# Mixture-of-experts layer after attention: every handoff of the expert pipeline one round apart, and eight result buffers

## The reference

```python
logits = x @ gate_weight.T                      # 128 tokens here per block, 1024 in all
probs = softmax(logits)
routing_weights, selected_experts = top_k(probs, 8)
routing_weights = routing_weights / routing_weights.sum(-1)
for each expert e:                              # 64 experts, I = 96, H = 256
    gate, up = split(x @ gate_up_weights[e])    # 256 -> 2 * 96
    out = (silu(gate) * up) @ down_weights[e]   # 96 -> 256
    final += combine[:, e] * out
x = x + final
```

## Time and profile before

| | us |
|---|---|
| median of 3 runs | 521.24 |
| lowest and highest | 520.41, 523.81 |
| span of the profiled execution | 576.6 |
| expert pipeline in the profile | about 325 to 547 |
| of it, full rounds back to back | 365 to 529 |
| reading back and adding, storing | 547 to 576.6 |
| PE, DVE, ACT, POOL busy | 477.4, 342.7, 305.9, 212.3 |

### The profile page before, as it was taken

One profiled execution on the slowest core, in us unless ns is written; L12 is line 12 of the kernel. 1 busy time (PEld: TensorE's weight loads), 2 busy tenths in 40 slices (PEclk: granted clock), 3 DMA queues, 4 the chain that ended last, 5 costly groups with the idle time before them and its releaser, 6 DMA issues. The chain is left out here.

```text
span 576.6 us, 10371 instructions
## 1 busy us (share of the span) xinstructions
PE 477.4 (83%) x3073; PEld 351.1 (61%) x3073; DVE 342.7 (59%) x1204; ACT 305.9 (53%) x854; POOL 212.3 (37%) x224
## 2 busy tenths in 40 slices
PE   4586999999899899999983766987988888888666
PEld 1366767877787678788653423765665666655322
DVE  4768496596685894795793564544355454553033
ACT  3456787885966887779864201333244343444200
POOL 0344110041114631025584642245444455445600
PEclk9799999999999999999996788999899899899879
DMA  8920862000301102002998739884444444330097
GB/s 283 411 70 19 167 131 74 1 1 0 76 1 54 69 30 73 2 1 74 345 404 291 278 107 298 227 288 129 111 115 115 113 128 127 107 95 13 19 363 304
DMA packets 47318, 79.49 MB, mean 138 GB/s; under 512 B 8266, under 2 KB 31127, under 8 KB 46880
## 3 DMA queue, kind: packets, MB, share of 16 engines
q1 hardware_dynamic: 36864, 55.34, 31.1%
q0 software_dynamic: 7680, 16.93, 8.2%
q10 hardware_dynamic: 2720, 6.55, 3.5%
HBM read 56.54 MB, written 26.44 MB: 144 GB/s over the span
## 5 line engine op out<-in xcount | busy, mean ns | idle before, releaser
L620 POOL DMA_INDIRECT pair_rows<-eout,dest x93 | 91.8, 987 | 99.5 <-ACT eout L634 78.2
L833 ACT ACTIVATE sact<-ps 128x192 f32<-128x192 f32 (+1 forms) x50 | 16.3, 325 | 122.7 <-remote 73.6
L1323 DVE SCALAR_TENSOR_TENSOR aact<-sact,wcol,ps 128x96 f32<-128x96 f32 x96 | 26.0, 311 | 92.6 <-issue 87.1
L1685 PE MATMUL ps<-wts,xg 128*64 (+1 forms) x512 | 71.5, 342 | 3.7 <-DVE copy_gu L1346 2.2
L691 ACT ACTIVATE lg<-lg,mneg 128x128 f32<-128x128 f32 (+1 forms) x128 | 56.4, 443 | 26.1 <-DVE mneg L1029 21.5
L1685 PEld LDWEIGHTS ps<-wts,xg 128*64 128x64 f32 x512 | 53.0, 143 | 16.5 <-issue 9.5
L541 POOL DMA_INDIRECT slot_rows<-rows,pair_slot x48 | 47.9, 998 | 37.2 <-issue 24.1
L1512 PE MATMUL ps<-oT,wo_sb 128*128 128x256 f32 x240 | 54.4, 380 | 0.0
L1706 PE MATMUL ps<-wts,aT 96*64 96x256 f32 (+1 forms) x256 | 49.8, 395 | 4.4 <-issue 3.4
L1512 PEld LDWEIGHTS ps<-oT,wo_sb 128*128 128x128 f32 x240 | 44.6, 190 | 6.2 <-ACT oT L634 0.7
L634 ACT ACTIVATE lg<-lg,rinv 128x128 f32<-128x128 f32 (+1 forms) x128 | 45.9, 448 | 2.5 <-issue 1.7
(11 more groups left out here) (237 smaller groups left out, 1184.4 us busy)
## 6 DMA issues: line engine op xcount, KB each, us to landing
wts<-in_experts_dram SPq DMA_DIRECT2D x22, 640.0 KB, 8.0
xrow<-slot_rows SPq DMA_DIRECT2D x192, 65.0 KB
pairs<-pair_rows SPq DMA_DIRECT2D x16, 512.0 KB, 11.2
wts<-in_experts_dram ACTq DMA_DIRECT2D x10, 640.0 KB, 6.1
slot_rows<-zero SPq DMA_DIRECT2D x1, 4160.0 KB, 24.2
wT<-in_wq_t_dram SPq DMA_DIRECT2D x4, 512.0 KB, 6.5
wq_raw<-in_wq_l_dram SPq DMA_DIRECT2D x1, 2048.0 KB, 14.6
wo_sb<-in_wo_l_dram SPq DMA_DIRECT2D x1, 2048.0 KB, 20.5
```

The lines of the kernel that those rows point to most:

```text
L620: nc.gpsimd.indirect_dma_start(out=pair_d, out_offset=bass.IndirectOffsetOnAxis(ap=dest[:, d:d + 1], axis=0), in_=out_rows(d), in_offset=N ...
L1685: ins = nc.tensor.matmul(ps[h * R:(h + 1) * R, 2 + u % 2, k * I2:(k + 1) * I2], xg[u % len(xg)][:, k, cc, h * R:(h + 1) * R], moving, star ...
```

## The change

The computation, the tiles and the weights stay. What changes is which round each step belongs to, the order within an iteration, and the buffers that this needs. PE now does, group by group in turns, `turn_rows` of round g and `gate_up` of g - 1, then `turn_act` of g - 2, then `down` of g - 3. ACT does `silu` of g - 1, `copy_turned` and `copy_down` of g - 2, `copy_out` of g - 3. DVE does for each group `copy_turned_rows`, `copy_gate_up` and `weigh`, and `find_rows` of both groups at the end. There is one more iteration. `sact` has two buffers; from the ninth group on `gate_up` goes through three PSUM banks (5, 2, 3) in turn, and `turn_act` through one bank (4) for the whole round; results have eight buffers instead of six.

```diff
-    NOUT = 6
+    NOUT = 8
...
+        round_of = {g: r for r, gs in enumerate(ROUNDS) for g in gs}
...
+        PLAIN = 8
+
+        def gu_bank(u):
+            return 2 + u % 2 if u < PLAIN else (5, 2, 3)[(u - PLAIN) % 3]
+
+        def gu_before(u):
+            return u - 2 if u < PLAIN else u - 3
...
             def copy_turned(a):
-                act.wait_ge(at_done, a + 1)
+                act.wait_ge(at_done, ROUNDS[round_of[a]][-1] + 1)
...
             def silu(u):
                 act.wait_ge(gu_done, u + 1)
-                if u >= 1:
-                    act.wait_ge(act_ready, u)
+                if u >= 2:
+                    act.wait_ge(act_ready, u - 1)
...
-            for g in range(NR + 2):
+            for g in range(NR + 3):
                 us = ROUNDS[g - 1] if 1 <= g <= NR else []
-                outs = ROUNDS[g - 2] if g >= 2 else []
-                for a in outs:
-                    copy_turned(a)
+                outs = ROUNDS[g - 2] if 2 <= g < NR + 2 else []
                 for u in us:
                     silu(u)
                 for a in outs:
+                    copy_turned(a)
+                for a in outs:
+                    copy_down(a)
+                for a in ROUNDS[g - 3] if g >= 3 else []:
                     copy_out(a)
-                for u in us:
-                    copy_down(u)
...
             for g in range(NR + 1):
                 ins_ = ROUNDS[g] if g < NR else []
-                for x in ins_:
-                    copy_turned_rows(x)
-                    find_rows(x)
                 us = ROUNDS[g - 1] if g else []
                 for k in range(max(len(us), len(ins_))):
+                    if k < len(ins_):
+                        copy_turned_rows(ins_[k])
+                        copy_gate_up(ins_[k])
                     if k < len(us):
                         dve.wait_ge(dest_ready, us[k] + 1)
                         weigh(us[k])
-                    if k < len(ins_):
-                        copy_gate_up(ins_[k])
+                for x in ins_:
+                    find_rows(x)
...
             def turn_act(a):
                 pe.wait_ge(act_ready, a + 1)
-                if a >= 2:
-                    pe.wait_ge(at_copied, a - 1)
-                if a == TABLE_AT:
-                    pe.wait_ge(cols_read, 2)
+                if a == ROUNDS[round_of[a]][0] and a:
+                    pe.wait_ge(at_copied, a)
...
             def gate_up(u):
-                if u >= 2:
-                    pe.wait_ge(act_ready, u - 1)
+                if u == PLAIN:
+                    pe.wait_ge(cols_read, 2)
+                if gu_before(u) >= 0:
+                    pe.wait_ge(act_ready, gu_before(u) + 1)
...
-            for g in range(NR + 2):
-                outs = ROUNDS[g - 2] if g >= 2 else []
+            for g in range(NR + 3):
...
-                for x in ROUNDS[g] if g < NR else []:
-                    turn_rows(x)
-                for a in outs:
+                xs = ROUNDS[g] if g < NR else []
+                us = ROUNDS[g - 1] if 1 <= g <= NR else []
+                for k in range(max(len(xs), len(us))):
+                    if k < len(xs):
+                        turn_rows(xs[k])
+                    if k < len(us):
+                        gate_up(us[k])
+                for a in ROUNDS[g - 2] if 2 <= g < NR + 2 else []:
                     turn_act(a)
-                for u in ROUNDS[g - 1] if 1 <= g <= NR else []:
-                    gate_up(u)
-                for a in outs:
+                for a in ROUNDS[g - 3] if g >= 3 else []:
                     down(a)
```

More of the change, by code:

```diff
@@ L214, in adaln_attn_ffn @@
         o = 16 * KIB
-        xg = [at(f"xg{i}", [P, 2, CC, P], off) for i, off in enumerate((take(2 * KIB), take(2 * KIB), r3 + 10 * KIB, rows_off[0] + NOUT * KIB))]
+        xg = [at(f"xg{i}", [P, 2, CC, P], off) for i, off in enumerate((take(2 * KIB), take(2 * KIB), r3 + 10 * KIB, rows_off[0] + (NOUT - 2) * KIB))]
         wcol = at("wcol", [P, (NE + MORE) // 2], take(384))
-        sact = at("sact", [P, 2, I], take(2 * I * 4))
+        sact = [at(f"sact{i}", [P, 2, I], off) for i, off in enumerate((take(2 * I * 4), row_off + 2 * KIB))]
         aact0 = take(2 * I * 4)
@@ L233, in adaln_attn_ffn @@
         assert o <= spare + 5 * KIB
-        eout = at("eout", [P, NOUT, C], rows_off[0])
+        eout_pair = [at(f"eout{i}", [P, 2, C], off) for i, off in enumerate([rows_off[0] + 2 * i * KIB for i in range(NOUT // 2 - 1)] + [row_off])]
         eout_first = at("eout_first", [P, 3, C], r3 + 12 * KIB)
@@ L822, in copy_turned @@
                 n = len(GROUPS[a])
-                act.wait_ge(at_done, a + 1)
+                act.wait_ge(at_done, ROUNDS[round_of[a]][-1] + 1)
                 if a >= 2:
                     act.wait_ge(dn_done, a - 1)
-                copy(aT[a % 2][0:I, 0:n, :], ps[0:I, 4 + a % 2, 0:n * P].rearrange("p (k t) -> p k t", k=n)).then_inc(at_copied, 1)
+                copy(aT[a % 2][0:I, 0:n, :], ps[0:I, 4, a % 2 * 2 * P:(a % 2 * 2 + n) * P].rearrange("p (k t) -> p k t", k=n)).then_inc(at_copied, 1)
             def silu(u):
@@ L830, in silu @@
                 act.wait_ge(gu_done, u + 1)
-                if u >= 1:
-                    act.wait_ge(act_ready, u)
-                nc.scalar.activation(sact[:, 0:n, :], ps[:, 2 + u % 2, 0:n * I2].rearrange("p (k i) -> p k i", k=n)[:, :, 0:I],
+                if u >= 2:
+                    act.wait_ge(act_ready, u - 1)
+                nc.scalar.activation(sact[u % 2][:, 0:n, :], ps[:, gu_bank(u), 0:n * I2].rearrange("p (k i) -> p k i", k=n)[:, :, 0:I],
                                      ACT.Silu).then_inc(silu_done, 1)
@@ L845, in copy_out @@
                 else:
-                    copy(eout[:, d % NOUT:d % NOUT + n, :], ps[:, 6 + a % 2, 0:n * C].rearrange("p (k c) -> p k c", k=n)
+                    copy(eout_pair[d % NOUT // 2][:], ps[:, 6 + a % 2, 0:n * C].rearrange("p (k c) -> p k c", k=n)
                          ).then_inc(out_copied, 1)
@@ L1322, in weigh @@
                 for k, d in enumerate(GROUPS[u]):
-                    ins = V.scalar_tensor_tensor(out=aact[u % 2][:, k, :], in0=sact[:, k, :], scalar=wcol[:, d:d + 1],
-                                                 in1=ps[:, 2 + u % 2, k * I2 + I:(k + 1) * I2], op0=ALU.mult, op1=ALU.mult)
+                    ins = V.scalar_tensor_tensor(out=aact[u % 2][:, k, :], in0=sact[u % 2][:, k, :], scalar=wcol[:, d:d + 1],
+                                                 in1=ps[:, gu_bank(u), k * I2 + I:(k + 1) * I2], op0=ALU.mult, op1=ALU.mult)
                 ins.then_inc(act_ready, 1)
@@ L1644, in turn_act @@
                 pe.wait_ge(act_ready, a + 1)
[L1645 to L1648 removed]
+                if a == ROUNDS[round_of[a]][0] and a:
+                    pe.wait_ge(at_copied, a)
                 for k in range(len(GROUPS[a])):
[L1650 removed]
+                    ins = T_(ps[0:I, 4, (a % 2 * 2 + k) * P:(a % 2 * 2 + k + 1) * P], aact[a % 2][:, k, :])
                 ins.then_inc(at_done, 1)
@@ L1684, in gate_up @@
                                 moving = copy_gu[m % NCOPY][:, cc * I2:(cc + 1) * I2]
-                            ins = nc.tensor.matmul(ps[h * R:(h + 1) * R, 2 + u % 2, k * I2:(k + 1) * I2],
+                            ins = nc.tensor.matmul(ps[h * R:(h + 1) * R, gu_bank(u), k * I2:(k + 1) * I2],
                                                    xg[u % len(xg)][:, k, cc, h * R:(h + 1) * R], moving, start=(cc == 0), stop=(cc == CC - 1))
```

3 lines of the change are left out of this document (1 added, 2 removed).

## The result

Before: 521.4 us (median of 4, 520.41 to 523.81). After: **541.42 us** (median of 4, 540.07 to 542.75). The ratio is 1.034, interval 1.028 to 1.041: the change makes the kernel 20.0 us slower. The forecast was 536, in a range of 513 to 543.

What follows compares the result with a forecast made beforehand. The prediction took TensorE's own sequence of instructions to bound the timed rounds. From 521.2 us it added 12.8 for TensorE's order, took off 1 for handoffs and added 3.4 for the end: 536.4, say 536 us, range 513 to 543.

Steps and rivals of the forecast that it cites:

- The sum: Whole kernel: 521.2 + 12.8 for order, - 1 for handoffs, + 3.4 for the end, giving 536.4, say 536 us.
- Rival A: Faster: late completions are in timed runs too, looser handoffs regain idle time and switches lie in it; 511.5 us, chance 0.15.
- B: No change: another resource, likely SyncE's loads, sets rounds of about 6.5 us, only the end counts; 524.6 us, chance 0.17.
- Part 1: TensorE's order: six changes of form a round instead of two, 0.145 us each; rounds of 6.52 us, +12.8 us.
- Part 2: Handoffs: TensorE's waits for aact and copy_gu go, mostly absent from timed runs; -1 us, ends 0 and 4.9.
- Part 3: VectorE and ScalarE: same instructions reordered, later find_rows may delay row loads; 0, at worst 2 us.
- Part 4: End of the kernel: results leave one round later, last twelve scatters run back to back; +3.4 us, ends 0 and 6.

Runs made afterwards that it cites:

- before again: The kernel before, unchanged, run and profiled again; its profiled execution took 523.75 us, its group's median was 524.32 us.
- four further: The changed kernel, with TensorE alternating by double tile from the sixth iteration on, ten changes of form a round instead of six; 552.34 us, ratio 1.056.
- the buffers alone: The changed kernel with the old orders on all three engines, keeping its result and silu buffers and PSUM banks; 525.16 us, ratio 1.000.
- the alternation alone: The kernel before with only turn_rows and gate_up alternating by group on TensorE, four changes of form a round; 527.43 us, ratio 1.005.
- the depth alone: The changed kernel without alternation, turn_act ahead of gate_up, find_rows directly behind copy_turned_rows, down still of round g - 3; 533.93 us, ratio 1.019.
- The run without alternation: The changed kernel, but TensorE does turn_rows of both groups, then gate_up of both; four changes of form a round; 537.77 us, ratio 1.022.
- the run with two switches: The changed kernel, but TensorE does turn_rows of both groups, turn_act, gate_up of both, down; two changes of form a round; 535.55 us, ratio 1.021.
- the exception: The kernel before with turn_rows and gate_up alternating by group in the first eight iterations only; start 30.7 us, 523.64 us, ratio 0.998.
- the run with early copies: The changed kernel, with ScalarE copying a group's results directly behind copy_turned, ahead of the copies of down weights; 537.18 us, ratio 1.025.
- the run with the end first: The changed kernel, but from iteration NR - 2 on down and copy_out of round g - 3 stand first on their engines; 543.72 us, ratio 1.038.

## Why the prediction was right, and where not

**The sum.** Between the profiles of before again and after the span grows by 16.3 us: start -2.8, 21 rounds of 0.54 more +11.4, end +7.3, the rest +0.4. The forecast was made of +12.8 - 1 + 3.4 = +15.2. The three measurements gave +20.0, +15.4 and +15.6. The first is the highest because both medians lay apart there (521.4 for before against 524.0 to 524.9 later, 541.4 against 539.4 to 540.5); why, stays open.

**What bounds the kernel.** Right: the 55 us of the first profile were its own, the timed rounds are TensorE's sequence of 5.94 us. Rival A fell with that, and so did B: rounds of 6.5 would have been there before.

**Part 1, the order on TensorE.** Right in mechanism and size: the round forecast at 6.52 measured 6.52 and 6.51, the change 0.147 against 0.145. It holds for two more (0.31 a round), four more (0.54, by single rounds 0.58) and four further (0.59); with two fewer than after the round is 6.23 as well, and waits raise the mean to 6.34. The 22nd round is counted in the start; 21 of 0.58 make 12.2, not 12.8. The change from gate_up to transposes, which before had not shown, costs with the change back 0.30 us, as the nearest rows did (0.16 and 0.13). Changing the tiling mode drains the engine, says the Trainium skill (TensorEngine Tiling (Array Packing), Key Properties). The runs agree in that each change costs time, 0.15 us for these fp32 matmuls; that a drain is what it consists of, they don't show.

**Part 2, the handoffs.** Forecast -1, and about that much was gained. Before again waits once in the rounds counted here, 1.2 us for xg; the profile of after does not, and its 21 rounds grew by 11.4 us and not by 12.2. Which part of the change removes this wait is not shown: it is still there with the buffers alone (1.0 us), with the alternation alone (0.9) and with the depth alone (1.1). More than 1.6 us there was not to give back.

**Part 3, VectorE and ScalarE.** Right for after: from 363 us on TensorE does not wait for xrow in its first two profiles, and for 0.8 us in the third. The run without alternation waits 1.0 us there and the run with two switches 2.9; the depth alone, with find_rows early, does not. Whether find_rows or chance made these waits is open.

**The start.** "In the first rounds the time goes by the arrival of rows and is kept" failed: after was 2.8 us shorter there than before again. The arrival of rows does bind, but gate_up of the round before stands between the two turn_rows now and fills part of the wait. It is argued from the starts in thirteen profiles, with one exception, and not shown. Three of the longer starts (the exception, two switches, depth alone) also hold some 3 to 6 us at the lower clock, at waits for rows or right behind them.

**Part 4, the end.** The term was mis-sized: +3.4, with ends 0 and 6, measured **+7.3 to +7.5**, outside its own bounds. I counted what stands between the third last round's other steps and its down (turn_act, gate_up, a change: 3.2 us), but a later place in the order also moves it past that round's own length. In before again this down starts 5.05 us ahead of the end of the last gate_up, in after 0.57 behind it. TensorE's timelines, before again and after:

```profile
476.92 0.38 PE L1706 MATMUL ps<-wts,aT 96*64 x1
...
479.32 2.82 PE L1685 MATMUL ps<-wts,xg 128*64 128x192 f32 x32
...
481.97 0.38 PE L1706 MATMUL ps<-wts,aT 96*64 x1
```

```profile
486.63 2.77 PE L1694 MATMUL ps<-wts,xg 128*64 128x192 f32 x32
489.34 0.64 PE L1396 MATMUL ps<-ident,aact 128*96 128x128 f32 x4
489.91 0.43 PE L1715 MATMUL ps<-wts,aT 96*64 x1
```

That is 5.6 us, of which the forgotten part is a down (1.83) and a turn_act (0.57).

How long the end is, GpSimd's timelines tell. Before again scatters twelve tiles back to back, from 479.37, 1.74 us ahead of the silu from which the end is measured (481.11); after scatters sixteen, from 490.19, 0.39 behind it (489.80). Four more at 1.29 us are 5.2 us and the later start is 2.1, together 7.3. So the sum also had the number of scatters wrong: it let the last twelve start as soon as their results are there, but they queue behind the four of the round ahead of them. Those come late by ScalarE's queue, which I had not counted at all: 1.7 us by the run with early copies, where sixteen still run back to back but start at 486.60, 1.33 ahead of the silu.

That neither the alternation nor the buffers nor find_rows make the long end is shown: it is 12.4 in all four kernels with down at g - 2, and 19.7 to 19.9 with it at g - 3 as long as the end was left alone. But those at g - 3 all have ScalarE's new order, and those at g - 2 its old one. Beyond the 1.7 us the runs don't part the two.

So the sum fits because its errors nearly cancel: the end was 3.9 too low and the start 2.8 too high, while the rounds with the handoffs are off by only 0.4 (11.8 forecast, 11.4 measured). That much of it is luck. The time, 541.4, is 5.4 over the forecast and 1.6 under the top of the range; without the shorter start, which nobody forecast, it would be outside. No kernel that ran is shown to beat the one before.

## What to carry to other kernels

When TensorE has no idle time, its order is a cost of its own: count the changes between full-width and column-tiled matmuls in a round before loosening a handoff, and group the steps by form. A pipeline that is one round deeper gives little where little waited (1.6 us here), and at the end it shifts the last results on every engine that they queue on: count there how many pieces will stand in the slowest queue, and from when, in both orders. And profile the kernel before twice if its span is far from its times.

## What the runs showed of the hardware

One profiled execution was 55 us longer than the timed runs (span 576.6), with completions of TensorE reaching the other engines late; the same kernel profiled again had 521.9 and none of it. On TensorE a change between the full-width transposes and the matmuls on 64 columns and back costs 0.30 us: 0.10 ahead of the transposes, 0.15 in them, 0.05 behind. In the run with the end first, TensorE's granted clock fell to 0.51 within an idle time of 2.84 us in the midst of a busy stretch, for 6.8 us; with the depth alone it fell to 0.50, for 6.7 us, at the second of three waits of 0.92 to 0.94 us.
